# Expert products of an attention-and-experts kernel in split factors: weights split during the attention, five experts kept on chip

## The reference

```python
# attention: q, k are 16 wide per head, v 64 wide
out = (tril(phi(q) phi(k)^T) v + phi(q) phi(k_enc)^T v_enc) / denominator
x = layernorm(x + out @ Wout.T)
# experts: top-1 of 8, weighted with gate = p1 / (p1 + p2)
hmid = gelu(x @ w1[e] + b1[e])      # 256 -> 1024
hout = hmid @ w2[e] + b2[e]         # 1024 -> 256
x = layernorm(x + hout * gate)
```

## Time and profile before

| | |
|---|---|
| median of 3 runs | 1171.72 us (1170.37 to 1172.6) |
| the profiled execution | 1172.99 us, of which its span is 1171.2 us |
| TensorE busy | 1074.8 us (92% of the span) |
| VectorE busy | 582.8 us (50%) |
| ScalarE busy | 507.4 us (43%) |
| GpSimd busy | 474.4 us (41%) |
| mean granted TensorE clock | 0.957 of full |

### The profile page before, as it was taken

The page is one execution under the profiler, slowest core; times in us unless marked ns, Lnnn a source line. Parts: engine busy times, 40 slices in busy tenths (PEclk is TensorE's granted clock), DMA queues, the critical chain, the costliest instruction groups (busy, mean ns, idle before and its releaser), DMA issues. The chain is left out here.

```text
span 1171.2 us, 18689 instructions
## 1 busy us (share of the span) xinstructions
PE 1074.8 (92%) x6320; PEld 647.5 (55%) x6321; DVE 582.8 (50%) x963; ACT 507.4 (43%) x891; POOL 474.4 (41%) x507
## 2 busy tenths in 40 slices
PE   5799999999999999999999999973689999999994
PEld 4344465555546546546545555563356676676673
DVE  5386753663573572573555457537124334334332
ACT  2566635644654563663564554400213323323321
POOL 1364533443343452453444345300144444444442
PEclk9799999999999999999999999985789999999997
DMA  5733641642651462453354252104920110110010
GB/s 203 268 123 106 201 149 64 209 139 67 213 172 54 165 193 82 168 173 111 102 179 146 76 187 75 36 18 180 390 83 28 34 33 29 35 32 27 30 29 0
DMA packets 54789, 135.03 MB, mean 115 GB/s; under 512 B 6750, under 2 KB 10848, under 8 KB 52418
## 3 DMA queue, kind: packets, MB, share of 16 engines
q1 hardware_dynamic: 50978, 124.81, 31.8%
q0 software_dynamic: 3744, 9.31, 2.6%
HBM read 87.73 MB, written 47.29 MB: 115 GB/s over the span
## 5 line engine op out<-in xcount | busy, mean ns | idle before, releaser
L376 ACT ACTIVATE w<-slot 128x1024 f32<-128x1024 f32 (+1 forms) x256 | 231.0, 915 | 180.8 <-PE slot L723 180.7
L500 DVE SCALAR_TENSOR_TENSOR w<-w,mask 128x256 f32<-128x256 f32 (+1 forms) x192 | 176.5, 919 | 189.6 <-ACT w L376 179.7
L744 PE MATMUL osum<-w,values 128*64 128x512 f32 (+3 forms) x1280 | 251.3, 488 | 1.0 <-DVE w L503 1.0
L343 POOL TENSOR_TENSOR wsum<-w 128x512 f32<-128x512 f32 x64 | 96.6, 1509 | 365.7 <-DVE w L503 365.7
L1158 ACT ACTIVATE active<-upT,b 128x128 f32<-128x128 f32 x312 | 84.9, 383 | 156.9 <-PE upT L1236 156.8
L347 POOL TENSOR_TENSOR wsum<-wsum,w 128x768 f32<-128x768 f32 x64 | 122.7, 1917 | 62.9 <-DVE w L503 61.1
L1212 PE MATMUL down<-w,active 128*128 x624 | 144.4, 385 | 2.5 <-ACT active L1158 2.5
L1224 PE MATMUL up<-w,rowsT 128*128 x312 | 143.5, 603 | 0.7 <-ACT rowsT L1147 0.7
L503 DVE TENSOR_SCALAR w<-w 128x768 f32<-128x768 f32 (+2 forms) x192 | 141.2, 735 | 0.0
L723 PE MATMUL slot<-qop,kop 64*128 64x512 f32 (+3 forms) x640 | 126.0, 424 | 9.9 <-issue 7.7
L1212 PEld LDWEIGHTS down<-w,active 128*128 128x128 f32 x624 | 117.7, 193 | 18.7 <-issue 3.8
(11 more groups left out here) (187 smaller groups left out, 1168.2 us busy)
## 6 DMA issues: line engine op xcount, KB each, us to landing
kop<-k_rows SPq DMA_DIRECT2D x32, 640.0 KB, 5.6
qop<-q_rows SPq DMA_DIRECT2D x32, 512.0 KB, 7.3
w<-in_w SPq DMA_DIRECT2D x16, 1024.0 KB, 9.5
inv<-inv_rows SPq DMA_DIRECT2D x56, 256.0 KB, 4.4
k_rows<-kh SPq DMA_DIRECT2D x32, 320.0 KB
k_rows<-kl SPq DMA_DIRECT2D x32, 320.0 KB
q_rows<-qh SPq DMA_DIRECT2D x32, 256.0 KB
q_rows<-ql SPq DMA_DIRECT2D x32, 256.0 KB
```

Of the source, the lines that this page charges most:

```text
L343: pool.tensor_tensor(dst[:, 0, :], src[:, 0, 0:N], src[:, 0, N:2 * N], ALU.add)
L376: act.activation(w[:, n % 2, :, at:at + cols], slot[u % 2][:, :, 0:cols], ACT.Square, bias=HALF_ROOT).then_inc(squared, 1)
L500: dve.scalar_tensor_tensor(src[:, :, 0:cut], src[:, :, 0:cut], 0.5, mask[:, 0:cut].unsqueeze(1).to_broadcast([P, 2, cut]), ALU.add, ALU.mu ...
L744: last = pe.matmul(osum[n % 2][HD * s:HD * s + HD, q0:N], values[:, j, h * HD:h * HD + HD], w[:, n % 2, s, at:at + N - q0], start=(u == 0) ...
```

## The change

Each expert's w1 and w2 are cut into eight pieces of 128 x 512 numbers (`PIECES`, `PW`). In the attention of sequence b the pieces of expert b are split: SyncE loads piece j into one of the two halves of `xT` (`load_part`), ScalarE copies it to `part_h` with rounding to fp32r (`part_high_of`, in the gaps of `HI_AT`), VectorE subtracts that from the piece in place (`part_low_of`, in the gaps of `LO_AT`), and SyncE writes both parts to the HBM tensor `w_parts` (`store_part`). There is one `part_h`, so the copy of a piece waits until the high part of the piece before has been stored (`high_out`) and its low part made. A half of `xT` is loaded again when its low part has been stored (`low_out`). The ring `att` has 13 buffers in place of 14.

The experts' weights are then loaded as high and low parts, 4 MB an expert in place of 2 MB. Five experts fit (`kept`); four are loaded in the routing, the fifth when the first has landed, and the sixth to eighth take the places of the first three when these experts' slots are done. `in_row` of the routing lies in the fifth place, and the routing has four more small VectorE operations (`place_of`, `slots_to`).

In a slot `up` and `down` are done as three fp32r products, so `up` has 12 matmuls of 512 columns and `down` 24 of 256 columns. ScalarE makes the high part of the turned rows and, in two halves after four GELUs each, of `active`; VectorE makes the low parts. `active` has one buffer in place of two.

```diff
-RING, ATT, INV = 4, 14, 4
+RING, ATT, INV = 4, 13, 4
...
+PIECES, PW = 8, 512
+HI_AT = {10: 0, 13: 1, 16: 2, 19: 3, 22: 4, 25: 5, 27: 6, 29: 7}
+LO_AT = {11: 0, 14: 1, 17: 2, 20: 3, 23: 4, 26: 5, 28: 6, 30: 7}
+KEPT = 5
...
+    w_parts = nc.dram_tensor("w_parts", [E, P, 2, PIECES, PW], F32).ap()
...
+        part_h = sb("part_h", [P, PW], F32R)
...
+                if b > 1:
+                    for r in range(2):
+                        sp.wait_ge(low_out[r], 16 * (b - 1) * PIECES // 2)
...
+            def load_part(b, j):
+                n = b * PIECES + j
+                if j < 2:
+                    sp.wait_ge(x_split, 2 * min(b + 2, B))
+                    if b == B - 1:
+                        sp.wait_ge(low_out[j], 16 * (n // 2))
+                else:
+                    sp.wait_ge(low_out[j % 2], 16 * (n // 2))
+                src = w1_in[:, b, j // 2, PW * (j % 2):PW * (j % 2) + PW] if j < 4 else \
+                    w2_in[:, b, 2 * j - 8:2 * j - 6, :].rearrange("p c d -> p (c d)")
+                sp.dma_start(xT[:, j % 2, :], src).then_inc(part_in[j % 2], 16)
+
+            def store_part(b, j):
+                n = b * PIECES + j
+                sp.wait_ge(part_high, n + 1)
+                sp.dma_start(w_parts[b, :, 0, j, :], part_h[:, :].bitcast(F32)).then_inc(high_out, 16)
+                sp.wait_ge(part_low, n + 1)
+                sp.dma_start(w_parts[b, :, 1, j, :], xT[:, j % 2, :]).then_inc(low_out[j % 2], 16)
...
+                load_part(b, 0)
+                load_part(b, 1)
                 gather(b, 3)
+                store_part(b, 0)
+                load_part(b, 2)
+                store_part(b, 1)
                 if b + 1 < B:
                     send(b + 1, 0)
+                load_part(b, 3)
+                store_part(b, 2)
+                load_part(b, 4)
+                if b + 1 < B:
                     gather(b + 1, 0)
+                store_part(b, 3)
+                load_part(b, 5)
+                store_part(b, 4)
+                load_part(b, 6)
                 if b > 0:
                     store_rows(b - 1)
+                store_part(b, 5)
+                load_part(b, 7)
                 if b + 1 < B:
                     send(b + 1, 1)
+                store_part(b, 6)
+                if b + 1 < B:
                     gather(b + 1, 1)
+                store_part(b, 7)
                 if b > 0:
                     load_rows(b)
...
+            def part_high_of(b, j):
+                n = b * PIECES + j
+                act.wait_ge(part_in[j % 2], 16 * (n // 2 + 1))
+                if n > 0:
+                    act.wait_ge(high_out, 16 * n)
+                    act.wait_ge(part_low, n)
+                act.activation(part_h[:, :], xT[:, j % 2, :], ACT.Copy).then_inc(part_high, 1)
...
+                    if g in HI_AT:
+                        part_high_of(b, HI_AT[g])
...
+            def part_low_of(b, j):
+                dve.wait_ge(part_high, b * PIECES + j + 1)
+                dve.tensor_tensor(xT[:, j % 2, :].bitcast(F32R), xT[:, j % 2, :], part_h[:, :].bitcast(F32),
+                                  ALU.subtract).then_inc(part_low, 1)
...
+                    if g in LO_AT:
+                        part_low_of(b, LO_AT[g])
...
-        w1 = sb("w1", [P, E, KD, I])
-        w2 = sb("w2", [P, E, IC, D])
+        kept = sb("kept", [P, KEPT, 2, PIECES * PW], F32R)
...
-LOADED_EARLY = 2
-
-
-def load_expert(sp, e, w1, w2, w1_in, w2_in, w_sem):
-    sp.dma_start(w1[:, e, :, :], w1_in[:, e, :, :]).then_inc(w_sem[e % 2], 16)
-    sp.dma_start(w2[:, e, :, :], w2_in[:, e, :, :]).then_inc(w_sem[e % 2], 16)
-
-
-def route(nc, ctx, sem, w_seq, table_loaded, w_sem, routed, w1, w2, b1, b2, w1_in, w2_in, b1_in, b2_in,
-          logits, tables, row_index, out_index, gates, expert_of):
+LOADED_EARLY = 4
+
+
+def load_expert(sp, e, kept, w_parts, w_sem):
+    half = PIECES * PW // 2
+    for c in range(2):
+        sp.dma_start(kept[:, e % KEPT, :, c * half:c * half + half].bitcast(F32),
+                     w_parts[e, :, :, c * PIECES // 2:(c + 1) * PIECES // 2, :].rearrange("p a j n -> p a (j n)"))\
+            .then_inc(w_sem[e], 16)
...
-    in_row = sb("in_row", [P, TT, P], F32R)
+    in_row = kept[:, KEPT - 1, 0, :].rearrange("p (t n) -> p t n", n=P)
...
+        after(dve.tensor_scalar(index_f[:, :], expert_f[:, :], float(KEPT), float(-KEPT), ALU.is_ge, ALU.mult))
+        after(dve.tensor_tensor(index_f[:, :], index_f[:, :], expert_f[:, :], ALU.add))
+        after(dve.tensor_copy(place_of[:, :], index_f[:, :]))
+        after(dve.tensor_copy(slots_to[:, :], last_slot[:, :]))
...
-        for e in range(LOADED_EARLY, E):
-            load_expert(sp, e, w1, w2, w1_in, w2_in, w_sem)
-            sp.wait_ge(w_sem[(e - 1) % 2], 32 * ((e - 1) // 2 + 1))
-            if e - 1 == LOADED_EARLY - 1:
-                sp.sem_inc(w_seq, LOADED_EARLY)
-            else:
-                sp.sem_inc(w_seq, 1)
-        sp.wait_ge(w_sem[(E - 1) % 2], 32 * ((E - 1) // 2 + 1))
-        sp.sem_inc(w_seq, 1)
+        for e in range(E):
+            sp.wait_ge(w_sem[e], 32)
+            sp.sem_inc(w_seq, 1)
+            ahead = e + LOADED_EARLY
+            if KEPT <= ahead < E:
+                done = sp.value_load(slots_to[0:1, ahead - KEPT:ahead - KEPT + 1], min_val=1, max_val=SLOTS)
+                sp.wait_ge(down_full, done)
+            if ahead < E:
+                load_expert(sp, ahead, kept, w_parts, w_sem)
...
+            e = expert(act, s)
+            act.wait_ge(w_seq, e + 1)
             act.wait_ge(turned_full, s + 1)
             if not (isinstance(s, int) and s < 2):
                 act.wait_ge(up_full, s - 1)
-            act.activation(rowsT[:, k % 2, :, :], turned[:, :].rearrange("p (k n) -> p k n", k=KD),
-                           ACT.Copy).then_inc(rowsT_ready, 1)
+            act.activation(rowsT_h[:, k % 2, :, :], turned[:, :].rearrange("p (k n) -> p k n", k=KD),
+                           ACT.Copy).then_inc(rows_high, 1)
 
         def body(s, k):
             if not (isinstance(s, int) and s == SLOTS - 1):
                 turn(s + 1, k + 1)
             e = expert(act, s)
             act.wait_ge(upT_full, s + 1)
-            if not (isinstance(s, int) and s < 2):
-                act.wait_ge(down_full, s - 1)
-            for c in range(IC):
-                act.activation(active[:, k % 2, c, :], upT[:, c * P:(c + 1) * P], ACT.Gelu,
-                               bias=b1[:, bass.ds(e * IC + c, 1)]).then_inc(active_ready, 1)
+            if not (isinstance(s, int) and s == 0):
+                act.wait_ge(active_ready, s * 2)
+            for half in range(2):
+                for c in range(half * IC // 2, (half + 1) * IC // 2):
+                    last = act.activation(active[:, c, :], upT[:, c * P:(c + 1) * P], ACT.Gelu,
+                                          bias=b1[:, bass.ds(e * IC + c, 1)])
+                last.then_inc(active_made, 1)
+                act.wait_ge(active_made, s * 2 + half + 1)
+                cs = slice(half * IC // 2, (half + 1) * IC // 2)
+                act.activation(active_h[:, cs, :], active[:, cs, :], ACT.Copy).then_inc(active_high, 1)
...
+        def rows_low(s, k):
+            dve.wait_ge(rows_high, s + 1)
+            dve.tensor_tensor(rowsT_l[:, k % 2, :, :], turned[:, :].rearrange("p (k n) -> p k n", k=KD),
+                              rowsT_h[:, k % 2, :, :].bitcast(F32), ALU.subtract).then_inc(rowsT_ready, 1)
...
+            if not (isinstance(s, int) and s == SLOTS - 1):
+                rows_low(s + 1, k + 1)
             if not (isinstance(s, int) and s == 0):
                 residual(s - 1, k - 1)
-
+            for half in range(2):
+                cs = slice(half * IC // 2, (half + 1) * IC // 2)
+                dve.wait_ge(active_high, s * 2 + half + 1)
+                dve.tensor_tensor(active_l[:, cs, :], active[:, cs, :], active_h[:, cs, :].bitcast(F32),
+                                  ALU.subtract).then_inc(active_ready, 1)
+
+        rows_low(0, 0)
...
+        def weights(r, part, at, cols):
+            return kept[:, bass.ds(r, 1), part, at:at + cols].rearrange("p o n -> p (o n)")
+
         def second(s, k):
-            e = expert(pe, s)
-            pe.wait_ge(active_ready, s * IC + IC)
+            r = place(s)
             if not (isinstance(s, int) and s < 2):
                 pe.wait_ge(down_read, s - 1)
             for c in range(IC):
-                last = pe.matmul(down[k % 2][:, :], active[:, k % 2, c, :], w2[:, bass.ds(e, 1), c, :].rearrange(
-                    "p o d -> p (o d)"), start=(c == 0), stop=(c == IC - 1))
+                if c % (IC // 2) == 0:
+                    pe.wait_ge(active_ready, s * 2 + 2 * c // IC + 1)
+                for n, (a, part) in enumerate(((active_h, 0), (active_h, 1), (active_l, 0))):
+                    last = pe.matmul(down[k % 2][:, :], a[:, c, :], weights(r, part, KD * I + c * D, D),
```

(12 more changed lines are left out.)

45 lines of the change are left out of this document (29 added, 16 removed).

## The result

The changed kernel takes 1299.97 us (median of 4 runs, 1294.73 to 1303.37) beside 1172.16 us for the kernel before: a ratio of 1.109, 95% interval 1.105 to 1.113. The forecast was slower, 1230 us, 1178 to 1275. So the sign was right and 70 us are missing. The profiled execution has a span of 1301.6 us against 1171.2, and a mean granted clock of 0.888.

A forecast was written before the change was run, and what follows sets the result against it. TensorE was taken to set the pace in attention and slots. From 1173.0 us profiled: less 32 (slots), plus 21 (piece 0), 59 (piece 7) and 10 (clock) gave 1231, as a median 1230; 8-in-10 range 1178 to 1275.

The forecast's parts named there:

- the boundaries: Passage from one sequence to the next: 59 us for piece 7's late copy and 10 us for the lower clock.
- What bounds the kernel: TensorE sets the pace, busy 700 of 718 us in the attention and 294 of 299 in the slots.
- Pace of the products: Slots: split products of 256 columns start 0.127 us apart, `down` takes 3.05 us, the slot 7.1; 32 us saved.
- Rival (b): Slots: a 256-column product takes 0.216 us as now, slots 9.1 us, 40 us longer in all: 1302 us; chance 0.05.
- (c): Slots gain nothing, the chain through both halves of `active` being 0.9 us longer than added: 1262 us; chance 0.07.
- The weights [...] end at about the same time: First slots and routing: 20 MB loaded from the start in place of 4 then 12, costed at nothing.
- the gather's slack: Slots: the next gather needs some 3 us to land, so a slot of 6.6 us would do.
- Piece 0: Attention, gap 12: late load delays the q copy 1.7 us, subtractions add 1.3; 21 us over seven sequences.
- The second term: Attention, gap 15: two VectorE subtractions stand ahead of the small `kl`, 1.3 us more a sequence.
- Piece 7: Gap 0: its copy waits for piece 6's high store behind the second send; 8.5 us a boundary, 59 in all.
- rival (a): Gap 0: the send does not hold up the store; 1.8 us a boundary, 13 in all, 1174 or 1160; chance 0.15.
- The clock: Behind each boundary pause TensorE works three us at half speed, losing 1.5 us: 10 us in all.

The follow-up runs named there:

- late_loads_small: Changed kernel with the loads of experts 5, 6 and 7 cut to one sixteenth of an expert each: 1278.3 us, run once.
- high6_first: Changed kernel with the store of piece 6's high part issued ahead of the sequence's second send, no longer behind it: 1260.4 us.
- high6_mid: Changed kernel with the store of piece 6's high part issued in the middle of the second send, behind its four q stores: 1253.7 us, run once.

## Why the prediction was right or wrong

The sign was right, by the mechanism that the forecast named. The time was wrong by 70 us, from four places: the boundaries 90.5 for 69 (21.5 us), piece 0 with gaps 8 to 16 40.4 for 21 (19.4), sequence 0 9.1 for nothing, the slots 10.5 in place of 32 (21.5). Two of the steps are failed ones, the loads costed at nothing and the sequence not looked at; in the other two places the mechanism was right and a size was off.

- **What bounds the kernel**: right. In the traces the time lost is TensorE's waits and its lower clock.
- **Pace of the products**: right. `down` 2.95 for 3.05, slot 7.15 for 7.1. Rival (b), by which 256 columns cost 0.216 us, is out at 0.118, and (c) too.
- **"The weights [...] end at about the same time", costed at nothing**: wrong, the step that failed in the slots. True of the loads at the start, but three of 4 MB come inside the loop, beside the gathers; I had checked the gather's slack (it lands 3 us after issue, a slot of 6.6 would do) for a quiet DMA. They cost 16 us, and late_loads_small gets 14.8 of them back; the other slots with a mean of 7.26 for 7.1 cost another 5.
- **Piece 0**: the chain right, 1.7 us for a sequence measured as about 2.3, but the clock behind this pause was left out. 40.4 us for 21; the extra idle is some 16, the rest is work at 0.50. In the five other traces with this attention it is 26 to 31, again some 14 to 18 of them idle, so half of the miss or more belongs to one execution and the term itself was near. The second term (1.3 for `kl`) did not show in the changed kernel and did as soon as the first was gone.
- **Piece 7**: the mechanism right in each link, shown by high6_first and high6_mid. Mis-sized: 75 us of idle time for 59, by the landing of piece 5's store (4.0 for 2.6) and by "12.1 us" for the send, which took 15.6 (16.3 in the kernel before); with the store behind it 16.4 for 14.1. That SyncE itself needs 9.3 us for the eight issues was in no term, and rival (a) had 4.8 for them. Rival (a), by which the store passes the send, is out within one queue: the store landed 7.1 us after its issue and not 2.8, behind the last of the send.
- **The clock**: 1.5 a boundary measured as 2.2, and it falls behind the shorter pauses too. In the trace some 40 us of the 128 are work at the lower level: 15.5 at the boundaries, some 24 in gaps 8 to 16 (21 to 26 in all in the five others).
- **Sequence 0**: the forecast has no term for it. 9.1 us, since piece 3's load stands behind the first send, whose backlog the short gaps of that sequence don't cover (ScalarE stands 9.1 us before the copy of piece 3).
- **The range** ended at 1275, since it stacked upper ends for known terms only (77 + 24 + 35) and held nothing for a term that was overlooked.

## What to carry to other kernels

When work on a shared in-order queue is added, follow every item behind it, in the shortest iteration as well, and every transfer of other queues that it will run beside. Put what an engine waits for ahead of bulk transfers; count the time that the issuing engine needs for the bulk, and read how long it takes from its last landing, not from a rate in a window of it. Price a pause of 3 to 4 us on TensorE above its length, for the clock behind it: here some 16 us of extra idle time cost 26 to 31 us, and once 40. One stall hides the next: the gain of removing one is known only when the next has been looked for. And compare a stretch that no edit touched in every trace at hand before a few us of one trace are given a cause.

## What the runs showed of the hardware

- After pauses of 3.3 and 3.9 us the granted clock stood at 0.50 for 12 us of work and more in one sequence and came back within 6 in another: beside the idle time the first cost 8 us, the second 2.5. Six traces have seven such pauses each; the long stretch follows two of the 42, one of them also of 3.9 us.
- A 256 KB store landed 3.5 us after issue when issued just before a send of 2.36 MB, and 6.0 to 7.6 us after issue beside a send under way, in the send's queue; through another queue 5.9 to 9.6, median 6.5.
- The first three transfers of a send are issued in 0.58 us each, the later ones take 1.1 to 1.7, 9.3 us for eight (567.75 to 577.00). A store behind them in the same queue landed over 16 us after the send's start.
- VectorE's subtraction of 128x512 went from 0.69 to 1.09 us beside a product of GpSimd of 0.61.
- Split products start 0.118 us apart at 256 columns, 0.235 at 512 and 0.11 at 128: from 512 to 256 they nearly halve, from 256 to 128 they hardly fall.
